# Output projection as rounded products per pair, shared projection banks, and a new order at the end of a supertile and in the FFN, in a gated linear-attention layer on one Trainium2 core

## What is computed

```
xn   = layernorm(x) * gamma + beta
Q, K, V = xn @ W^T + b              # 1024 wide: 16 heads of 64
gate = silu(xn @ Wg^T + bg)
h_t  = alpha * h_(t-1) + k_t v_t^T ;  o_t = q_t h_t      # per head, alpha = sigmoid(alpha_logit)
x1   = layernorm(x + x + (o * gate) @ WO^T + bO)
gf   = sigmoid(... gelu(mean_t(x1) @ gc_w1 + gc_b1) ...)  # one number per batch
out  = x1;  three times:
    tf  = sigmoid(gelu(gelu(gelu(out @ w1+b1) @ w2+b2) @ w3+b3) @ w4+b4)
    out = out + (0.1 + range * (0.7 gf + 0.3 tf - 0.5) * 2) * twist(out)   # twist: quarters swapped, signs
y    = layernorm(x1 + out)
```

## Time and profile before

| | us |
|---|---|
| median of 3 runs (1919.38 to 1921.05) | 1919.58 |
| the profiled execution | 1920.54 |
| its span, first to last instruction | 1918.8 |
| PE busy in it | 1836.1 (96%) |
| DVE busy | 1081.2 (56%) |
| ACT busy | 711.3 (37%) |
| POOL busy | 315.5 (16%) |

### The profile page before, as it was taken

How to read it: one execution, slowest core, us unless ns; L and a number is a source line. 1 busy time by engine, 2 the same in 40 slices (tenths; PEclk the granted TensorE clock), 3 DMA queues, 4 the chain that set the end, 5 groups by cost and what they waited for, 6 DMA issues and landing times.

```text
span 1918.8 us, 44137 instructions
## 1 busy us (share of the span) xinstructions
PE 1836.1 (96%) x19178; PEld 1408.3 (73%) x19178; DVE 1081.2 (56%) x2230; ACT 711.3 (37%) x1297; POOL 315.5 (16%) x246
## 2 busy tenths in 40 slices
PE   5999999999799999999989999999979999999996
PEld 4888888853588888884378888888338888888732
DVE  7646465644764655554665556565376565555546
ACT  3424242434442424234443233333444333324344
POOL 3111111102211111210221212021022021211002
PEclk9999999999899999999989999999999999999998
DMA  4000000000100000000010000000001000000001
GB/s 158 2 12 2 13 2 12 3 0 1 56 2 12 2 12 2 12 2 1 0 56 2 12 2 13 1 13 1 1 11 46 2 13 2 13 2 13 1 0 45
DMA packets 23345, 26.65 MB, mean 14 GB/s; under 512 B 3184, under 2 KB 22000, under 8 KB 23152
## 3 DMA queue, kind: packets, MB, share of 16 engines
q1 hardware_dynamic: 21152, 19.62, 3.2%
q10 hardware_dynamic: 2000, 4.20, 0.6%
HBM read 15.42 MB, written 8.39 MB: 12 GB/s over the span
## 4 chain that ended last, share of the span: by engine, by line
PE 87%; DVE 10%; ACT 2%; issue 1%; DMA 0%; POOL 0%; DVEq 0%; ACTq 0%; SPq 0%
PE bank L803 38%; PE bank L875 12%; PE bank L1029 8%; PE bank L866 7%; PE bank L830 6%; PE bank L857 6%; DVE x_nf L764 4%; PE bank L847 3%; DVE v_sb L771 3%; PE bank L839 3%; PE bank L1072 1%; DVE cpl L760 1%; PE bank L794 1%; DVE stats L557 1%; PE bank L1046 1%; PE bank L885 1%
## 5 line engine op out<-in xcount | busy, mean ns | idle before, releaser
L415 ACT ACTIVATE q_sb<-q_sb,pows 128x384 f32<-128x384 f32 (+2 forms) x387 | 168.7, 498 | 450.4 <-DVE q_sb L599 450.4
L721 DVE TENSOR_TENSOR o_g<-bank,gate 128x512 f32<-128x512 f32 x128 | 88.5, 691 | 438.4 <-PE bank L866 438.4
L345 POOL TENSOR_TENSOR k_end<-k_sc,pows 128x512 f32<-128x512 f32 x129 | 136.0, 1054 | 779.9 <-DVE k_sc L590 779.9
L433 ACT ACTIVATE h_bd<-h_seq,pows 64x256 f32<-64x256 f32 x256 | 129.9, 507 | 349.8 <-DVE h_seq L699 346.6
L875 PE MATMUL bank<-wo,o_g 128*128 128x256 f32 x1024 | 226.3, 379 | 0.0
L875 PEld LDWEIGHTS bank<-wo,o_g 128*128 128x128 f32 x1024 | 193.3, 190 | 26.1
L683 DVE COPY_PREDICATED att<-causal,bank 128x1024 f32<-128x1024 int32 x128 | 168.2, 1314 | 8.5 <-PE bank L830 8.0
L857 PEld LDWEIGHTS bank<-q_sb,h_bd 128*128 128x128 f32 x1024 | 134.1, 191 | 10.6
L866 PE MATMUL bank<-att,v_sb 128*64 128x128 f32 x2048 | 140.1, 279 | 0.0
L857 PE MATMUL bank<-q_sb,h_bd 128*128 128x128 f32 x1024 | 134.8, 275 | 0.0
L1029 PE MATMUL bank<-v_sb,f_w 128*128 128x512 f32 x256 | 118.4, 605 | 12.7 <-DVE v_sb L771 12.7
(11 more groups left out here) (136 smaller groups left out, 3351.8 us busy)
## 6 DMA issues: line engine op xcount, KB each, us to landing
x_in<-in_x SPq DMA_DIRECT2D x17, 512.0 KB, 4.0
out_y<-o_g SPq DMA_DIRECT2D x16, 512.0 KB, 2.9
v_sb<-in_wq ACTq DMA_DIRECT2D x1, 1024.0 KB, 5.0
v_sb<-in_wk SPq DMA_DIRECT2D x1, 1024.0 KB, 5.7
o_g<-in_wg ACTq DMA_DIRECT2D x1, 1024.0 KB, 9.3
o_g<-in_wv ACTq DMA_DIRECT2D x1, 1024.0 KB, 12.1
wo<-in_wo ACTq DMA_DIRECT2D x1, 1024.0 KB, 16.0
bias_v<-in_bV SPq DMA_DIRECT2D x1, 512.0 KB, 8.1
```

Source lines behind the costliest of these rows:

```text
L345: nc.gpsimd.tensor_tensor(k_end[:].rearrange("p (a z) (b r) -> p a (z b) r", z=2, r=BL), k_sc[:].rearrange("p (a z) (b r) -> p a (z b) r", ...
L415: last = nc.scalar.activation(q_sb[:, p % 2, d].rearrange("p (a z) n -> p a (z n)", z=2)[:, :, reach], q_sb[:, p % 2, 0].rearrange("p (a z ...
L433: nc.scalar.activation(h_bd[rows, :, e * DH:(e + 1) * DH], h_seq[rows, :, :], ACT.Copy, scale=pows[rows, p, HP:HP + 1]).then_inc(s_hbd, 1)
```

## The change

1. **Output projection.** `wo` is split into `wo_hi` and `wo_lo` once. `o_g` shrinks to two pairs; ScalarE makes `o_hi` of it (`o_high`), GpSimd the rest `o_lo` (`o_low`), both two pairs deep. `y_part(p)` now is 12 rounded products of 128x256, three per chunk of 128 tokens, in banks 6 and 7, and is issued in the following pair behind the projections; that of pair 7 behind g(0) of the next supertile.
2. **Banks.** k and q alternate between banks 0 and 1, and g goes where k was, so it waits for the keys' evacuation. State updates move to bank 4, all `k_end` transposes too. The value products use banks 2, 3, 5, 1, 2, 3, 0, 5.
3. **Supertile end.** The input transposes move from pair 7 to pair 6, `x_parts` on ScalarE with them; k(0) of the next supertile goes ahead of `from_chunk(7)`; q(0) and g(0) follow it; `y_part(7)` is last. The transposes of x1 move to pair 0 of the next supertile, 4 sets per batch in place of 5. After the last supertile no projection or load for a successor is made. VectorE evacuates the first two value products ahead of `norm_apply`.
4. **FFN.** The first layer of visit n+1 is cut in four: tile 0's halves on both sides of layer 3, tile 1's both behind layer 4. `h1` holds one group only and lies in `q_sb[:, 1]`.

```diff
-        o_g = sb("o_g", [P, NP, ST])
+        o_g = sb("o_g", [P, 2, ST])
+        o_hi = sb("o_hi", [P, 2, ST], f32r)
+        o_lo = sb("o_lo", [P, 2, ST], f32r)
...
+        def k_bank(p):
+            return p % 2
+        def q_bank(p):
+            return 1 - p % 2
+        def g_bank(n):
+            return n % NP % 2 if n else 5
...
-            order += [(2, n, range(GT))] + [(1, n + 1, [0])] * more + [(3, n, range(GT))] + [(1, n + 1, [1])] * more
-            order += [(4, n, range(GT))]
+            order += [(2, n, range(GT))] + [(1, n + 1, [(0, 0)])] * more
+            order += [(3, n, range(GT))] + [(1, n + 1, [(0, 1)])] * more
+            order += [(4, n, range(GT))] + [(1, n + 1, [(1, 0), (1, 1)])] * more
...
-            return bank[(2, 3, 1, 4, 5, 6, 7, 0)[m]]
+            return bank[(2, 3, 5, 1, 2, 3, 0, 5)[m]]
...
+            def o_low(p, n):
+                pool.wait_ge(s_ohi, n + 1 + C0)
+                nc.gpsimd.tensor_tensor(o_lo[:, p % 2], o_g[:, p % 2], o_hi[:, p % 2].bitcast(f32),
+                                        ALU.subtract).then_inc(s_olo, 1)
...
+            def o_high(p, n):
+                act.wait_ge(s_og, n + 1 + C0)
+                act.wait_ge(s_yp, n - 1 + C0)
+                nc.scalar.activation(o_hi[:, p % 2], o_g[:, p % 2], ACT.Copy).then_inc(s_ohi, 1)
...
                             tokens_of(n + 1, 4)
+                            if p == 0 and s:
+                                x1_copied(it - 1, 6)
+                            if p == NP - 2 and following:
+                                x_parts(it + 1, (0, 1))
+                            o_high(p, n)
                         else:
-                            x_parts(it + 1, (0, 1))
-                            queries_shifted(0, n + 1)
-                            act.wait_ge(s_og, n + C0)
-                            gate_of(0, n + 1)
+                            if following:
+                                queries_shifted(0, n + 1)
+                            o_high(p, n)
+                            if following:
+                                act.wait_ge(s_og, n + C0)
+                                gate_of(0, n + 1)
...
+            def y_part(p, n):
+                pe.wait_ge(s_olo, n + 1 + C0)
+                for c in range(NC):
+                    tok = slice(c * C, (c + 1) * C)
+                    dst = bank[6 + c // 2][:, (c % 2) * D:(c % 2 + 1) * D]
+                    for i, (l, w) in enumerate(((o_hi, wo_hi), (o_hi, wo_lo), (o_lo, wo_hi))):
+                        last = nc.tensor.matmul(dst, l[:, p % 2, tok], w[:, p, :], ...
...
                         if p + 1 < NP:
-                            project("k", p + 1, 0).then_inc(s_k, 1)
+                            project("k", p + 1, k_bank(p + 1)).then_inc(s_k, 1)
                             pe.wait_ge(s_gev, n + 1)
-                            project("g", p + 1, 7).then_inc(s_g, 1)
+                            project("q", p + 1, q_bank(p + 1)).then_inc(s_q, 1)
+                            pe.wait_ge(s_kev, n + 2 + C0)
+                            project("g", p + 1, g_bank(p + 1)).then_inc(s_g, 1)
...
+                        if p:
+                            y_part(p - 1, n - 1)
```

More of the change, by code:

```diff
@@ L180, in build @@
         s_og = sem("o_gated")
-        s_y = sem("y_ready")
+        s_ohi = sem("o_hi_made")
+        s_olo = sem("o_lo_made")
+        s_yp = sem("y_part_added")
+        s_wohi = sem("wo_hi_made")
+        s_wolo = sem("wo_lo_made")
+        s_y = sem("y_first_half_ready")
         s_r = sem("residual_sum_ready")
@@ L363, in _ @@
                     pool.sem_inc(s_xfree, 1)
-                    for p in range(NP - 1):
-                        ends_of(p + 1, it * NP + p + 1)
-                        if p == NP - 5:
+                    for p in range(NP):
+                        n = it * NP + p
+                        if p + 1 < NP:
+                            ends_of(p + 1, n + 1)
+                        elif following:
+                            ends_of(0, n + 1)
+                        o_low(p, n)
+                        if p == NP - 5 and following:
                             pool.wait_ge(s_stats, it + 2)
@@ L717, in _ @@
-                        dve.wait_ge(s_o, n + 1 + C0)
-                        dve.wait_ge(s_gev, n + 1)
-                        if p == 0:
-                            dve.wait_ge(s_out, b * NS * 16 + C0)
-                        nc.vector.tensor_tensor(o_g[:, p, :], bank[5], gate[:, p % 2, :],
-                                                ALU.mult).then_inc(s_og, 1)
-                    queries_of(0, (it + 1) * NP)
-                    for h in range(2):
-                        dve.wait_ge(s_y, it * 2 + h + 1)
+                        if p + 1 < NP:
+                            if p:
+                                masked(n)
+                            keys_of(p + 1, n + 1)
+                            if p == 0:
+                                dve.wait_ge(s_out, b * NS * 16 + C0)
+                                dve.wait_ge(s_wolo, 1)
+                            queries_of(p + 1, n + 1)
+                            if p == NP - 5 and following:
+                                input_stats(it + 1, b * STC + (2 * s + 1) * ST1)
+                            if p == NP - 3 and following:
+                                input_norm(it + 1, it * KT + C0)
+                            gated(p, n)
+                        else:
+                            if following:
+                                low_part(it + 1)
+                            masked(n)
+                            if following:
+                                keys_of(0, n + 1)
+                            gated(p, n)
+                            if following:
+                                queries_of(0, n + 1)
@@ L727, in _ @@
+                    for h in range(2):
+                        if h == 0:
+                            dve.wait_ge(s_y, it + 1)
+                        else:
+                            dve.wait_ge(s_yp, (it + 1) * NP + C0)
                         dve.wait_ge(s_x2b, it * 2 + 2)
                         nc.vector.tensor_tensor(x_2b[:, 2 * h:2 * h + 2, :], x_2b[:, 2 * h:2 * h + 2, :],
-                                                part(7 * (1 - h), 2), ALU.add).then_inc(s_r, 1)
+                                                part(6 + h, 2), ALU.add).then_inc(s_r, 1)
@@ L730, in _ @@
                     dve.wait_ge(s_r, it * 2 + 2)
-                    norm_stats(lambda c: x_2b[:, c, :], b * STC + (2 * s + 2) * ST1, s_r1)
-                    keys_of(0, (it + 1) * NP)
+                    norm_stats(lambda c: x_2b[:, c, :], b * STC + (2 * s + 1 + following) * ST1, s_r1)
+                    if s + 1 < NS:
+                        for m in range(2):
+                            values_kept(it + 1, m)
                     dve.wait_ge(s_rs1, it + 1)
@@ L900, in _ @@
             pe.wait_ge(s_xf, KT)
-            for n, (w, bk, done) in enumerate((("q", 1, s_q), ("k", 0, s_k), ("g", 7, s_g))):
+            for n, (w, bk, done) in enumerate((("q", q_bank(0), s_q), ("k", k_bank(0), s_k), ("g", g_bank(0), s_g))):
                 pe.wait_ge(s_wlo[n], 1)
@@ L1014, in _ @@
                     if layer == 1:
-                        for j in tiles:
+                        for j, m in tiles:
                             t = g * GT + j
@@ L1045, in _ @@
                             for k in range(2):
-                                last = nc.tensor.matmul(bank[4 + j], f_w2[:, k, :], h1[:, g * GT + j, k, :],
+                                last = nc.tensor.matmul(bank[4 + j], f_w2[:, k, :], h1[:, j, k, :],
                                                         start=(k == 0), stop=(k == 1))
```

254 lines of the change are left out of this document (129 added, 125 removed).

## The result

The changed kernel takes **1949.01 us** (median of 4 runs, 1947.71 to 1952.12) against 1919.58 of the kernel before on the same chip: ratio 1.0154, 95% interval 1.0136 to 1.0172. It is slower by 29.4 us; 31.4 had been forecast, with a range of 1908 to 1985. The profiled execution has a span of 1946.9 us and a mean granted clock of 0.976 (0.986 before).

The account below looks back on a forecast made before the run. TensorE, busy 96% of the span, was taken as the bound. Terms -33.8 -4.2 -1.0 -2.7 -16.0 +28.5 +42.0 +3.0 +7.0 +8.5 = +31.3 on 1920.5, less 1.0: 1951 us, range 1908 to 1985.

Parts of the forecast that it names:

- (a): Output projection: three rounded products at 0.122 us each replace one fp32 product of 0.432 us, 512 times: -33.8 us.
- fourth rival: Output-product weight loads stand in series with the products: 0.217 us a product, +146 us, 2097 us in all; chance 0.05.
- (b): Pairs 0 to 5: the 2.7 us chain through o_hi and o_lo is covered by TensorE's other work and costs nothing.
- (c): Pair 6: output products wait 1.9 us for o_lo, with x_f and x_hi ahead of o_hi on ScalarE; 15 times, +28.5 us.
- Rival 2: Waits in pairs 6, 7 set by rounding alone, not queues: both about 0, 1867 us, or 1909 with one; chance 0.14.
- (d): Pair 7: output products wait 2.8 us, as ScalarE queues the next supertile's shifted queries ahead of o_hi; 15 times, +42.0 us.
- (e) to (g): Old supertile end -4.2 and -1; g behind the keys' evacuation in their shared bank +3 and +7; starts -2.7 us.
- (h): FFN: the new order removes first-layer waits for the update and one final-transpose wait per batch; together -16 us.
- (i): TensorE clock: the 2.8 us waits make it fall to half speed at 5 of 15 supertile ends, +8.5 us.

Follow-up runs that it names:

- e5_ffn_alone: The kernel before with the new FFN order alone: 1896.84 us, ratio 0.9880.
- e4_fp32: The e3_both kernel with fp32 output products in the new places instead of rounded ones, without high and low parts: 1896.41 us, ratio 0.9878.
- e3_both: On the changed kernel, both moves: pair 5's output products behind pair 7's scores on TensorE, pair 7's o_hi ahead of next supertile's shifted queries on ScalarE: 1870.61 us.
- e2_ohi_first: On the changed kernel, ScalarE does pair 7's o_hi ahead of the next supertile's shifted queries instead of behind them: 1892.47 us, ratio 0.9859.

## Why the prediction held, and where it was off

The study splits the +29.4 us: FFN order -22.8 (before to `e5_ffn_alone`); supertile end, shared banks and starts -0.4 (to `e4_fp32`); rounded products with their remaining chain -25.8 (to `e3_both`); the two waits and their clock falls +78.4 (to the changed kernel). The second step is one comparison of medians, and its -0.4 is too small for the runs to tell from nothing. It also holds both moves, with fp32 products; what they do to those was not measured by itself.

- **(a) Products.** Forecast 0.122 us each, measured 0.119 to 0.120: 128 x (1.73 - 1.44) = -37 instead of -33.8. The cost went with the columns (the forecast's 0.117) more than with the instruction. The spacing of 0.12 at 128-wide loads also settles the fourth rival: loads of the same rows do overlap running products here. The sentence of the Trainium skill that they overlap only where the row group differs ("TensorE: Matmul & The Clock Gate", Part 3, "The mechanism") does not hold in this trace.
- **(b) Pairs 0 to 5 free.** Right: 32 waits, all in pairs 6 and 7.
- **(c) First wait.** Forecast 1.9, measured 1.69 plus 0.25 on the block behind it. The cause given, o_hi in ScalarE's queue behind x_f and x_hi, is only part of it. By the trace that queue held o_hi up for 0.33 us. Most of the wait is the data's own path, which the working of (c) left out: from the end of the chunk products at some 113.65 through gating, o_hi and o_lo to 116.69 are 3.0 us, and TensorE has only updates and scores beside it, 1.4. The number came out because the two paths end 0.3 us apart, so it owes something to luck. No run moved x_f and x_hi alone, so the 0.3 is read from the trace and not tested. In size, `o_lo` took 1.28 instead of 1.10, the steps ahead of it were about as much shorter, and TensorE's own work was 0.15 longer. Rival 2 had this path, with a slip: its 0.8 + 0.62 + 1.10 and two hand-overs are the 2.7 us of (b), which against 1.4 leave 1.3 and not 0. Its 1922 - 55 doesn't follow from its terms either, as (c) and (d) are 70.5.
- **(d) Second wait.** Forecast 2.8, measured 2.65 plus 0.25, and `e2_ohi_first` gives 2.79 back for each. The queue is the cause, as forecast: 2.89 us between o_g and o_hi, and the wait goes with the exchange. That one exchanged call was worth 56 us, which the working of (d) contained (the queue order) and didn't draw as a conclusion.
- **(e) to (g).** Forecast together -4.2 - 1 + 3 + 7 - 2.7 = +2, measured -0.4. For g behind the keys in pair 0 the forecast of 0.45 has its row: the load at 526.44 waits 0.41, the 18 projections take 4.60 instead of 4.38 us; half of it, 0.2 x 16 = 3.5 us, reaches the time, and in middle pairs nothing. At the very start there is a loss that no term had: g waits 1.95 us for the keys, whose evacuation stands behind the slow state copy of the last section.

```profile
526.44 0.19 PEld L876 LDWEIGHTS bank<-x_hi,wg_hi 128*128 128x128 f32 x1 [0.41 <-DVE k_sc L642]
```

- **(h) FFN.** Forecast -16, measured -22.8. The mechanism was right, the term too small. The waits as TensorE's list has them in the kernel before are 12.7 us, and the final transposes' are 31.5 before, 29.9 in `e5_ffn_alone`: 14 of the 22.8. The rest is mostly what a wait costs beside its listed length. The first products of the second layers of visits 1 to 5 start 14.08, 13.60, 13.53, 14.15 and 14.15 us after those of the visit ahead, and 14.18 and four times 12.76 in `e5_ffn_alone`. That is 4.3 us a batch, 17 in all, for 12.7 us of waits, so a wait costs about 0.7 us and not its 0.53. From a batch's last second layer to the next batch's first it is another 1.0 to 1.7 us less.

```profile
PE bank L1029 <- DVE v_sb L771: 12.7, 24, 0.6
```

- **(i) Clock.** This is the term that failed: 5 falls forecast, 11 at the 15 hand-overs measured, 11 x 1.55 = +17, and 3 more for those of the last supertile and the start, against +8.5. The step at fault took the waits of 2.8 us alone, as the ones that are long enough, and put a fall behind a third of them. In the changed kernel 4 of the 11 falls sit behind the first wait, of 1.69 us. That the falls follow the waits is shown: a fall at 12, 2 and 0 of the 15 hand-overs where only the second, only the first, or neither wait was left.

(c) and (d) together came to 15 x (1.15 + 2.79) = 59.1, and 4.4 + 1.4 that no move took away: 65 for 70.5. So the sum came within 2 us by luck, because its errors have both signs: about -3 (a), -6 (c, d), -2 (e to g) and -7 (h) against +11 for the clock and +4 at the start and in the last supertile.

## What to carry to other kernels

Splitting an fp32 product in three rounded ones is worth 0.07 us per 128x256 here, but it puts two operations on other engines ahead of each product: follow the queue of each of these engines to the last block of the loop, where no other work is left as cover, before counting the gain. Count beside it the data's own path from the product that makes the input, since a free queue doesn't shorten that. A wait of one engine at a loop's end can be one exchanged pair of calls in another engine's program, as the second wait here was; try that before moving the waiting work. And a TensorE wait that comes once a period can cost more than itself: here a clock fall worth another 1.55 us came in 11 of 15 periods with both waits, in 12 with the longer alone, in 2 with the shorter alone.

## What the runs showed of the hardware

**VectorE stands still beside some work of GpSimd.** Where GpSimd's `o_lo` (115.42 to 116.69) runs, VectorE's `x_lo`, which reads two fp32 operands, starts at 115.75 and takes 2.02 us instead of 1.22: it ends at 117.77, some 1.1 us after GpSimd, nearly its whole own duration. One state copy of the first pairs takes twelve times the usual 0.18 us beside an addition on GpSimd:

```profile
45.34 2.40 POOL L395 TENSOR_TENSOR x_2b<-x_2b,x_in 128x1024 f32<-128x1024 f32 x1
45.64 2.15 DVE L759 COPY h_seq<-h_st 128x64 f32<-128x64 f32 x1
```

It ends at 47.79, 0.05 us after GpSimd's operation. This reads as waiting for the other's end, not as sharing. Not every operation is held: VectorE's gating, which reads one operand from PSUM, takes 0.69 us beside GpSimd's k_end (121.80 and 121.60) as it does alone. And GpSimd loses little: its `o_lo` takes 1.26 to 1.30 us in all 128 cases. The Trainium skill says so ("SBUF — State Buffer", "Who interferes with whom"): a VectorE instruction with two SBUF inputs contends with a GpSimd instruction that reads SBUF, a VectorE copy in one of its faster 2-port modes contends with GpSimd too, and whichever issues first has the shared ports for its whole instruction. The durations here agree: 1.22 against 2.01 us, 0.18 against 2.15, and 9.81 us for five operations of 128x8 beside two of GpSimd. Whether the copy was in that mode no run shows.

**The clock fell behind short waits.** In `e2_ohi_first` only the first wait stands; two of its 15 hand-overs show a fall. One of them, in stretches of 3 us, with the wait of 1.68 us ahead of the product at 1315.27:

```profile
1314.00:1317.00 3.00, 1.73 (x9) 1.73 (x10) 2.96 (x4) 1.01 (x2) 1.22 (x1) 0.75 0.03 5
1317.00:1320.00 3.00, 3.00 (x17) 2.87 (x17) 0.51 (x1) 0.00 (x0) 0.00 (x0) 0.68 0.00 0
```

The other thirteen have the same wait and no fall; what tells them apart stays open.
